# Dilation of four graphs: one drop, one check and one set of right sides for a quad, with ranks scaled by a reciprocal

## The reference

```
h = h @ W + b;  nh = h / max(norm(h), EPS)
cos = nh @ nh.T;  ew = edge_weight * cos
h = ew @ h            (relu but for the last)
```

```
row = carry[n];  num = sum(row)
sf = where(num > 10, (num + 1) // 2, 1)
rm = row & (cumsum(row) % sf == 0)
rm = where(mask[n] != 0 and num > 1, rm, False)
carry[n] = row & ~rm;  carry[:, n] = carry[:, n] & ~rm
```

## Time and profile before

| | us |
|---|---|
| median of 3 runs | 3010.84 |
| lowest, highest | 3008.5, 3018.25 |
| the profiled execution, its own time | 3018.62 |
| its span, first to last instruction | 3016.8 |
| PE busy in the span | 2784.0 (92%) |
| DVE busy | 2277.1 (75%) |
| ACT busy | 1251.4 (41%) |
| POOL busy | 1082.2 (36%) |

### The profile page before, as it was taken

One profiled execution on the slowest core, in us unless ns is written; L12 is line 12 of the kernel. 1 busy time (PEld: TensorE's weight loads), 2 busy tenths in 40 slices (PEclk: granted clock), 3 DMA queues, 4 the chain that ended last, 5 costly groups with the idle time before them and its releaser, 6 DMA issues. The chain is left out here.

```text
span 3016.8 us, 41011 instructions
## 1 busy us (share of the span) xinstructions
PE 2784.0 (92%) x13446; PEld 1740.0 (58%) x13446; DVE 2277.1 (75%) x6124; ACT 1251.4 (41%) x3652; POOL 1082.2 (36%) x493
## 2 busy tenths in 40 slices
PE   6988999998999998899998997799999979999997
PEld 4655656655555655556655564455555545555786
DVE  4788998888988898898888886766566524676567
ACT  2544541545541554541554530233332224443564
POOL 4534333434333232321000000776666612443661
PEclk9999999999999999999999998899999989999998
DMA  6446336446327345326214102355554516996653
GB/s 215 134 136 206 105 99 213 137 130 210 109 84 227 113 133 192 105 62 190 91 57 164 60 15 98 128 212 215 191 188 181 189 70 242 396 395 270 241 200 126
DMA packets 304077, 492.27 MB, mean 163 GB/s; under 512 B 18544, under 2 KB 196080, under 8 KB 303856
## 3 DMA queue, kind: packets, MB, share of 16 engines
q1 hardware_dynamic: 303856, 489.57, 46.8%
HBM read 422.38 MB, written 67.11 MB: 162 GB/s over the span
## 5 line engine op out<-in xcount | busy, mean ns | idle before, releaser
L478 POOL TENSOR_SCALAR a_AT<-a_ats 128x512 uint8<-128x512 f32 x256 | 504.2, 1974 | 871.2 <-DMA a_ats<-in_adjT 809.3
L538 PE MATMUL a_acc<-a_ew,a_Hr 128*128 128x512 f32 x1536 | 796.0, 600 | 3.1 <-ACT a_hT L626 3.1
L717 DVE TENSOR_TENSOR a_ew<-adj,a_cos 128x512 f32<-128x512 f32 x768 | 522.6, 681 | 146.4 <-PE a_cos L531 145.2
L529 PE MATMUL a_cos<-a_nh 128*128 128x512 f32 x768 | 447.3, 582 | 2.4 <-DVE a_nl L709 2.4
L1286 POOL TENSOR_TENSOR b_dsum<-adj 128x1024 f32<-128x1024 f32 x16 | 141.9, 8870 | 662.2 <-DVE adj L1240 662.2
L538 PEld LDWEIGHTS a_acc<-a_ew,a_Hr 128*128 128x128 f32 x1536 | 292.3, 191 | 73.3 <-DVE a_ew L717 3.6
L640 ACT ACTIVATE a_vr<-a_D,a_sm_b,a_sm_sc 128x128 f16<-128x128 f32 x560 | 210.6, 456 | 246.0 <-DVE a_sm_b L766 245.4
L531 PE MATMUL a_cos<-a_nh,a_nl 128*128 128x512 f32 x768 | 306.3, 399 | 0.0
L530 PE MATMUL a_cos<-a_nl,a_nh 128*128 128x512 f32 x768 | 305.9, 398 | 0.0
L1130 PE MATMUL b_acc<-adj,b_h 128*128 128x512 f32 x512 | 224.3, 596 | 22.5 <-DVE adj L1240 22.5
L1290 POOL TENSOR_TENSOR b_dsum<-b_dsum,adj 128x1024 f32<-128x1024 f32 x96 | 225.8, 2352 | 14.1 <-POOL b_dsum L1290 0.5
(11 more groups left out here) (204 smaller groups left out, 4756.6 us busy)
## 6 DMA issues: line engine op xcount, KB each, us to landing
adj<-in_adjT SPq DMA_DIRECT2D x108, 1024.0 KB, 12.7
adj<-in_adjT SPq DMA_DIRECT2D x128, 512.0 KB, 5.8
a_ats<-in_adjT SPq DMA_DIRECT2D x256, 256.0 KB, 3.4
a_af<-in_adj SPq DMA_DIRECT2D x256, 256.0 KB, 3.4
scr_keep<-a_kp SPq DMA_DIRECT2D x128, 128.0 KB, 1.8
b_kp<-scr_keep SPq DMA_DIRECT2D x16, 1024.0 KB, 8.2
c_zi<-scr_z SPq DMA_DIRECT2D x32, 512.0 KB, 6.1
c_ai<-scr_ag SPq DMA_DIRECT2D x32, 512.0 KB, 7.0
```

Source lines behind the costliest of these rows:

```text
L478: e.tensor_scalar(AT[i][:, 4 * h:4 * h + 4, blk(k)].bitcast(U8), ats[h][:], 0.0, ONE8, ALU.is_gt, ALU.mult).then_inc(T["at"], 1)
L529: e.matmul(cos[j][:], n[:, blk(k)], n[:, half(j)], start=True, stop=False)
L538: e.matmul(acc[j][:], Hr[u % 2][:, k, :], ew[idx % 3][:], start=(k == 0), stop=(k == NK - 1)).then_inc(E["agg"], 1)
L717: e.tensor_tensor(ew[idx % 3][:], adj[g % 2][:, k, half(j)], cos[j][:], ALU.mult).then_inc(E["ew"], 1)
```

## The change

The small tiles of four graphs become one tile with an axis for the graph (AT, R, Ab, Au, X, Sd, v8), and the values of the rule lie in one tile `small`. Three steps that were four operations become one of 128x512: the drop, the check, and the pair Au and X. For the drop a single number has to be compared for all four graphs, where sf was a column for each. So the rule computes iv = 1/sf, and ACT's scale is sc = min(iv, 1) * g: vr then equals 1 where it equalled sf. The same holds for row_out, whose column sf becomes the constant 1.0. The pair Au and X leaves the start and is a stage of its own, cross, of width 0.6, after the fourth start. The again of PE waits once, for the one drop.

```diff
@@ DilationPlan
             for i in range(Q):
                 add(1, "start", n, i)
+            add(0.6, "cross", n)
             for r in range(K):
...
 def ticks(n, r):
-    return 9 * round_of(n, r) + n + (1 if r else 0)
+    return 10 * round_of(n, r) + n + (1 if r else 0)
@@ pe, again
                     for i in range(Q):
-                        if i % 2 == 0:
-                            e.wait_ge(T["vr"], Q * rr + i + 2)
-                        e.wait_ge(T["sd"], Q * rr + i + 1)
-                        count(i, Sd[i][(r + 1) % 2][:])
+                        if i == 0:
+                            e.wait_ge(T["sd"], rr + 1)
+                        count(i, Sd[(r + 1) % 2][:, i, :])
@@ pe, wide
                     if i == 0:
-                        e.wait_ge(T["vr"], Q * rr + (2 if j == 0 else 4))
+                        e.wait_ge(T["sd"], rr + 1)
...
-                    if j == 0:
-                        e.wait_ge(T["sd"], Q * rr + i + 1)
@@ dve, start
-                    e.wait_ge(T["sign"], 8 * n + 2 * i + 2)
-                    if i:
-                        e.wait_ge(T["x"], Q * n + i)
-                    e.scalar_tensor_tensor(Au[:], ab[:, blk(k)], 0.0, C["tri"][:], ALU.max, ALU.mult,
-                                           saturate=False).then_inc(T["au"], 1)
-                    e.wait_ge(T["au"], Q * n + i + 1)
-                    e.scalar_tensor_tensor(X[i][:], AT[i][:, k, blk(k)], 2.0, Au[:], ALU.mult, ALU.subtract,
-                                           saturate=False).then_inc(T["x"], 1)
+                elif kind == "cross":
+                    n, = a
+                    k, first = n % NK, Q * (n % 2)
+                    if n:
+                        e.wait_ge(T["v8"], n)
+                    e.wait_ge(T["sign"], 8 * n + 8)
+                    e.scalar_tensor_tensor(Au[:], Ab[:, first:first + Q, blk(k)], 0.0,
+                                           C["tri"][:].unsqueeze(1).to_broadcast([128, Q, 128]), ALU.max, ALU.mult,
+                                           saturate=False).then_inc(T["au"], 1)
+                    e.wait_ge(T["au"], n + 1)
+                    e.scalar_tensor_tensor(X[:], AT[:, :, k, blk(k)], 2.0, Au[:], ALU.mult, ALU.subtract,
+                                           saturate=False).then_inc(T["x"], 1)
@@ dve, rule
-                    e.scalar_tensor_tensor(sm["sc"][:], flat4, 10.5, mv, ALU.is_gt, ALU.mult).then_inc(T["ru"], 1)
-                    e.scalar_tensor_tensor(sm["va"][:], flat4, 1.5, mv, ALU.is_gt, ALU.mult).then_inc(T["ru"], 1)
+                    e.scalar_tensor_tensor(sm["g"][:], flat4, 10.5, mv, ALU.is_gt, ALU.mult).then_inc(T["ru"], 1)
                     e.wait_ge(T["ru"], t0 + 2)
                     e.tensor_scalar(sm["sf"][:], sm["t"][:], MAGIC, MAGIC, ALU.add, ALU.subtract).then_inc(T["ru"], 1)
-                    e.wait_ge(T["ru"], t0 + 3)
+                    e.scalar_tensor_tensor(sm["va"][:], flat4, 1.5, mv, ALU.is_gt, ALU.mult).then_inc(T["ru"], 1)
+                    e.wait_ge(T["ru"], t0 + 4)
+                    e.reciprocal(sm["iv"][:], sm["sf"][:]).then_inc(T["ru"], 1)
+                    e.wait_ge(T["ru"], t0 + 5)
+                    e.scalar_tensor_tensor(sm["h"][:], sm["g"][:], -4.0, sm["va"][:], ALU.mult, ALU.add).then_inc(T["ru"], 1)
+                    e.wait_ge(T["ru"], t0 + 6)
+                    e.scalar_tensor_tensor(sm["sc"][:], sm["iv"][:], 1.0, sm["g"][:], ALU.min, ALU.mult).then_inc(T["ru"], 1)
+                    e.wait_ge(T["ru"], t0 + 8)
                     e.tensor_tensor(sm["c"][:], sm["sc"][:], base0, ALU.mult).then_inc(T["ru"], 1)
-                    e.wait_ge(T["ru"], t0 + 4)
-                    e.scalar_tensor_tensor(sm["h"][:], sm["sc"][:], -4.0, sm["va"][:], ALU.mult, ALU.add).then_inc(T["ru"], 1)
-                    e.wait_ge(T["ru"], t0 + 7)
-                    e.tensor_tensor(sm["b"][:], sm["sf"][:], sm["h"][:], ALU.mult).then_inc(T["ru"], 1)
-                    e.wait_ge(T["ru"], t0 + 8)
-                    e.tensor_tensor(sm["b2"][:], sm["b"][:], sm["c"][:], ALU.add).then_inc(T["ru"], 1)
+                    e.wait_ge(T["ru"], t0 + 9)
+                    e.tensor_tensor(sm["b2"][:], sm["c"][:], sm["h"][:], ALU.add).then_inc(T["ru"], 1)
@@ dve, drop
-                    for i in range(Q):
-                        e.wait_ge(T["vr"], Q * rr + i + 1)
-                        e.scalar_tensor_tensor(Sd[i][(r + 1) % 2][:], vr[:, i, :], sm["sf"][:, i:i + 1], X[i][:],
-                                               ALU.is_equal, ALU.is_lt, saturate=False).then_inc(T["sd"], 1)
+                    e.wait_ge(T["vr"], Q * rr + Q)
+                    e.scalar_tensor_tensor(Sd[(r + 1) % 2][:], vr[:], 1.0, X[:], ALU.is_equal, ALU.is_lt,
+                                           saturate=False).then_inc(T["sd"], 1)
@@ dve, check
+                    e.scalar_tensor_tensor(Au[:], Sd[0][:], 1.0, Sd[1][:], ALU.mult, ALU.not_equal,
+                                           accum_out=C["flags"][:, n:n + 1], saturate=False).then_inc(T["v8"], 1)
@@ dve, row_out
-                    e.scalar_tensor_tensor(R[i][:, k, half(j)], v[c % 3][:], sm["sf"][:, i:i + 1],
+                    e.scalar_tensor_tensor(R[:, i, k, half(j)], v[c % 3][:], 1.0,
```

More of the change, by code:

```diff
@@ L386, in layer0 @@
         ss, s2, s3, rn = (P.sb(n, [128, NK]) for n in ("rnss", "rns2", "rns3", "rnrn"))
-        AT = [P.sb(f"AT{i}", [128, NK, N], FP8) for i in range(Q)]
-        R = [P.sb(f"R{i}", [128, NK, N], FP8) for i in range(Q)]
+        AT = P.sb("AT", [128, Q, NK, N], FP8)
+        R = P.sb("R", [128, Q, NK, N], FP8)
         ats = [P.sb(f"ats{i}", [128, 4, 128]) for i in range(2)]
         af = [P.sb(f"af{i}", [128, 512]) for i in range(3)]
-        Ab = [P.sb(f"Ab{i}", [128, N], FP8) for i in range(2 * Q)]
-        Au = P.sb("Au", [128, 128], FP8)
-        X = [P.sb(f"X{i}", [128, 128], FP8) for i in range(Q)]
-        Sd = [[P.sb(f"Sd{i}{j}", [128, 128], FP8) for j in range(2)] for i in range(Q)]
-        v8 = P.sb("v8", [128, 128], FP8)
+        Ab = P.sb("Ab", [128, 2 * Q, N], FP8)
+        Au = P.sb("Au", [128, Q, 128], FP8)
+        X = P.sb("X", [128, Q, 128], FP8)
+        Sd = [P.sb(f"Sd{j}", [128, Q, 128], FP8) for j in range(2)]
+        v8 = P.sb("v8", [128, Q, 128], FP8)
         base = P.sb("base", [128, 2, 2, 2])
@@ L402, in layer0 @@
         kp = [P.sb(f"kp{i}", [128, N], FP8) for i in range(2)]
-        sm = {n: P.sb(f"sm_{n}", [128, Q]) for n in ("t", "sf", "sc", "va", "h", "b", "c", "b2")}
+        small = P.sb("small", [128, 9, Q])
+        sm = {n: small[:, x, :] for x, n in enumerate(("t", "sf", "iv", "g", "sc", "va", "h", "c", "b2"))}
         Dp = P.ps("D", [128, 2, 512])
@@ L550, in pe @@
                     for q in others:
-                        e.matmul(rank(i)[:, 132:134], AT[i][:, q, blk(k)], (C["two1"] if q < k else C["zero1"])[:],
+                        e.matmul(rank(i)[:, 132:134], AT[:, i, q, blk(k)], (C["two1"] if q < k else C["zero1"])[:],
                                  start=(q == others[0]), stop=(q == others[-1]))
-                    count(i, AT[i][:, k, blk(k)])
+                    count(i, AT[:, i, k, blk(k)])
                 elif kind == "again":
@@ L633, in act @@
                         e.wait_ge(T["rw"], 8 * (n - 2) + 2 * i + 2)
-                    e.activation(Ab[Q * (n % 2) + i][:, half(j)], af[r % 3][:], ACT.Sign,
+                    e.activation(Ab[:, Q * (n % 2) + i, half(j)], af[r % 3][:], ACT.Sign,
                                  saturate=False).then_inc(T["sign"], 1)
@@ L637, in act @@
                     n, r = a
-                    e.wait_ge(T["ru"], ticks(n, r) + (10 if r == 0 else 9))
+                    e.wait_ge(T["ru"], ticks(n, r) + (11 if r == 0 else 10))
                     for i in range(Q):
@@ L650, in act @@
                     e.activation(v[c % 3][:], Dp[:, j, :], ACT.Abs,
-                                 bias=b1[:, i:i + 1] if j else sm["b"][:, i:i + 1],
+                                 bias=b1[:, i:i + 1] if j else sm["h"][:, i:i + 1],
                                  scale=sm["sc"][:, i:i + 1]).then_inc(T["av"], 1)
@@ L655, in act @@
                             e.wait_ge(T["av"], 8 * (n - 1) + 2 * i + 2)
-                        e.activation(b1[:, i:i + 1], Dp[:, 0, 511:512], ACT.Identity, bias=sm["b"][:, i:i + 1],
+                        e.activation(b1[:, i:i + 1], Dp[:, 0, 511:512], ACT.Identity, bias=sm["h"][:, i:i + 1],
                                      scale=sm["sc"][:, i:i + 1]).then_inc(T["b1"], 1)
@@ L804, in dve @@
                         e.wait_ge(T["tr"], 2 * m + j + 1)
-                        e.scalar_tensor_tensor(kp[m % 2][:, half(j)], Dp[:, j, :], 0.5, R[i][:, q, half(j)],
+                        e.scalar_tensor_tensor(kp[m % 2][:, half(j)], Dp[:, j, :], 0.5, R[:, i, q, half(j)],
                                                ALU.is_lt, ALU.is_gt, saturate=False).then_inc(T["kp"], 1)
```

25 lines of the change are left out of this document (7 added, 18 removed).

## The result

| | before | after |
|---|---|---|
| median of four runs, us | 3010.76 | 3116.43 |
| lowest, highest | 3008.5, 3018.25 | 3109.91, 3122.72 |
| ratio | | 1.0346 (1.0318 to 1.0374) |
| profiled execution, its span | 3018.62, 3016.8 | 3109.91, 3108.1 |
| DVE busy in the span | 2277.1 (75%) | 2174.8 (70%) |

The changed kernel is 3.5% slower. The forecast of 3044 us had the sign right, and 3116 lies above its whole range. DVE lost 102 us of work, and the time grew by 105. Behind layer 0 nothing changed: 1153 to 1154 us from there to the end of the span, both times.

The account below looks back on a forecast made before the run. In layer 0 PE and DVE are both near their limit, and ACT paces the drops in most rounds. 34 + 38 + 10 - 20 - 14 - 12 - 3 = +33 us on 3010.84 gives 3044 us, range 2990 to 3085.

Parts of the forecast that it names:

- absorbed: DVE's idle time in the rounds, waiting for cos, eats part of the delays: -20 us.
- The picture of the loop: Layer 0 rounds: ACT's Abs pace the drops; the new loop needs 4.3 us, PE's work 3.5 us a round.
- Part 3: PE's four counts after the drop all come after one semaphore, the last one 0.17 us later: +10 us.
- Part 4, Au and X: Merged pair in its own slot: 42 us of DVE instead of 68, half of the saving in PE-late starts: -12 us.
- Part 4, the check: Four check operations become one, 19 us less on DVE; its slot is then PE's, so -14 us kept.
- Part 1: Rule block on DVE: ten operations and a longer chain, 1.35 us instead of 1.11, 140 times: +34 us.
- Parts 2 and 3: Merged drop waiting for the fourth Abs, +38 us, and PE's counts after one semaphore, +10 us.
- Parts 1 to 3: Rule block, drop and counts in the rounds of layer 0 together: +82 us gross.
- The clock rival: PE's longer gaps in the rounds double the time at 1.2 GHz: some +25 us more, 3070 us; chance 0.1.
- The column of 256 row_out: row_out drops its column scalar, 15 us in all at the middle value, mostly hidden by waits for PE: -3 us.
- 82 - 11 - 40 - 50: Nearly even rival: delays absorbed twice as much, cheaper merged operations, full Part 4 savings: about 3005 us; chance 0.13.

Follow-up runs that it names:

- e13: e12 with the one merged drop of the change, counts and first wide waiting for it: 3060.08 us, 1.0149.
- e12: e10 with a rule of eleven small operations, one more, whose chain is one step shorter: 3004.54 us, 0.9966.
- e9: e5 with each first wide matmul waiting only for its own graph's drop: 3039.85 us, 1.0082.
- e5: e2 with the stage cross at width 0: 3060.14 us, 1.0147.
- e6: The kernel before with the change's new rule alone (ten operations, comparisons with 1.0), four drops and four checks: 3027.48 us, 1.0037.
- e10: e9 with Au and X computed for each graph in its start again and no stage cross: 3026.41 us, 1.0034.
- e2: The changed kernel with four drops of 128x128, PE's counts each waiting for their own: 3074.21 us, 1.0195.
- e1: The changed kernel with the stage cross at width 0 instead of 0.6: 3100.47 us, 1.0284.
- e11: The kernel before with Sd merged and one check of 128x512 instead of four: 3018.08 us, 1.0018.
- e4: The kernel before with an empty stage of width 0.6 after each block's fourth start: 3041.81 us, 1.0091.
- e7: The changed kernel with rule and drop widths of 1.15 instead of 0.9: 3083.02 us, 1.0231.

## Why the prediction was right in sign and wrong in size

| part | forecast, us | by the runs, us | which |
|---|---|---|---|
| drop and counts in the rounds | +48 | +36 | e13 against e12, stretch of the rounds |
| first wide waits for all four | 0 | +15 to +20 | the same, wide stretch; e9 against e5 |
| rule, with what its constant gives back | +34, -3 | +11 | e6 |
| Au and X merged, in a lump | -12 | +14 | e10 against e9 |
| width of the stage cross | 0 | +14 to +19 | e2 against e5, after against e1 |
| check merged | -14 | 0 to +5 | e11 |
| absorbed | -20 | in the rows above | |
| sum | +33 | +90 to +105 | measured +105 |

Taken one after the other from the changed kernel the steps close: cross at width 0 19 us, four drops 41, the wide's own waits 20, Au and X in the starts 14. These are 94 of the 105. What is left is e10, 10 us behind the kernel before, with the new rule and the merged check, and e6 with the rule alone has +11.

**Right.** The picture of the loop. The drop takes 0.69 us (forecast 0.68 to 0.76) and ends 0.73 us behind the last Abs, 0.34 later than four did (forecast 0.37). The rule block takes 1.36 (1.35). The shortest round with two slots is 4.14 (4.3): the counts and the way back to DVE take 0.52, not 0.68. The drop waits for a_vr in 116 rounds (120), for 133 us, above the 100 to 115. DVE's busy time fell by 102 us (80) without any gain, and the stages behind are unchanged. The sentence of the Trainium skill that speaks against the change ("Perfetto Trace Analysis", Optimizing Scalar/DVE Operations: where Vector isn't saturated but makes bubbles on other engines, breaking up instructions may let work be completed sooner) was the right one; the traces agree at 1, 2 and 4 pieces with 4.14, 3.87 and 3.73 us a round.

**The step of Part 3 that stopped too early.** "now all four come after one semaphore" was followed for the counts (L490) only. The wide matmuls wait on the same `sd`, and the diff changes their wait too. The view of the earlier trace rows had the row for it, 5.2 us at L575, but it is small just because the wide starts early, and I left it out. It needed a look at one last drop and the wide behind it, as above: 0.64 us ahead of its end. 15 to 20 us were missing. The +10 that Part 3 did put down isn't seen: from the last drop to the next rule block it is 0.52 us before and after.

**Part 4, Au and X: the wrong sign.** I summed DVE's work, 68 us against 42, and said that half of it was covered. The measured sign is the other one, +14 instead of -12. In the start shown DVE waits for cos, and it is PE that is late, so four small pairs can be free where a lump in a stage of its own is not. The text even had the reason ("start slots in which PE is late anyway") and then took a price for the merged pair as if it lay in the same slots.

**Part 4, the check.** The forecast kept 14 of 19 us. The measured gain is none. In the kernel before, PE starts the wide while DVE is still in its drops and is busy beside the check, which would cover DVE's work there; that reading wasn't tested by itself, and why merging may even lose 3 to 8 us is open.

**The stage without instructions.** "the cross now stands in a slot of its own" read the width as where the work stands. In this planner a width is also a share of 768 slots taken from all others. The forecast had no term for it; e4 prices it at 27 us in the kernel before with nothing in it, and e1 at 19 in the changed one. Which of the moved slots costs the time stays open.

**Part 1, too dear.** The duration was right, its sum of +34 was not the net: the same edit takes the column out of every drop, which shortens the paced loop by 0.06 us a round, 8 us in all. The prediction saw the column's price for row_out only (0 to 0.08, and the trace gave 0.06), and there it put down -3 of 15. Of the 27 us left in the rounds 15 came through in e6.

**Absorbed.** 20 of 82 us were to vanish in DVE's idle time. Of the shorter rule 17 and 21 of 25 us came through, of the longer one in e6 15 of 27, and of Parts 2 and 3 36 of 48. In sum the allowance was about right, in part by luck, since it splits otherwise than Parts 1 to 3 say.

**The clock rival.** It was given 3070 us if the time at the 1.2 GHz level doubled, for 25 us more. By the clock records of the traces it did double: 51 us up to the last mask before, 102 after. But it costs little here. These are PE's costliest groups, the matmuls of a_acc, before, after and in e4:

```profile
L538 PE MATMUL a_acc<-a_ew,a_Hr 128*128 128x512 f32 x1536 | 796.0, 600 | 3.1 <-ACT a_hT L626 3.1
```

```profile
L540 PE MATMUL a_acc<-a_ew,a_Hr 128*128 128x512 f32 x1536 | 804.2, 606 | 2.3 <-ACT a_hT L625 2.2
```

```profile
L539 PE MATMUL a_acc<-a_ew,a_Hr 128*128 128x512 f32 x1536 | 801.7, 604 | 1.9 <-ACT a_hT L627 1.9
```

With the three lines of a_cos added, the matmuls of the 768 slots are 14 us longer in PE's busy time after than before, 6 us in e4, and 4 us shorter in e13 than in e12. So by the profile, which models the ends of matmuls, the clock carries some 14 of the 105 us, 6 of e4's 27, and nothing of the merged drop's 55. The rest of the added time is idle time of PE. Inside the rounds the time at the lower level is 14 us before and 17 in e5; it is 37 in e2 (slots out), 41 in e1 (merged drop) and 63 after (both). So each of the two edits comes with a lower clock in the rounds, by about as much; which of PE's gaps bring it down was not looked at. e12 and e13 have 10 and 21.

**Sums that don't come out.** The column of 256 row_out at the middle value, 0.04 us, is 10 us and not 15, which is 0.06. 82 - 11 - 40 - 50 is -19, not -15. The ends of the forecast's own terms add up to -8 to +77, which is 3003 to 3088 and not 3010 to 3080. None of these reaches 3116.

The rows of the table miss 0 to 15 us of the measured 105, as the parts were measured on different bases: the merged drop gives 41 us between e5 and e1 and, without the wide's part, 36 on the fastest kernel. e7 shows that the loss also depends on how the widths fit.

## What to carry to other kernels

When several small operations are merged into one, ask for each input when it is ready and for each user when it starts: behind the slower producer here the last piece of four ends 0.3 us after it, the merged one 0.7, and a later user of the semaphore can pay as well, not only the next in line. A busy total that falls says nothing about the time: in each stretch look first at who is late there; work that lies in another engine's shadow is free in pieces and may be dear in a lump. In a schedule that deals out slots by weights, a new stage has a price even if it is empty, and a changed loop needs its weights set anew.

## What the runs showed of the hardware that was not expected

- A column as the scalar of a DVE operation costs 0.06 us against a constant: 763 against 701 ns at 128x512, 371 against 313 ns at 128x128 (the same fp16 and fp8 tiles, means over 256 and 560).
- The reciprocal of 128x4 takes 178 ns, as much as a product or a sum of two tiles of that size (177 and 178).
- In a block of 128x4 operations a dependent step weighs more than an operation: ten in a chain of seven take 1.37 us, eleven in a chain of six 1.19, nine in a chain of five 1.11.
- PE's time at the 1.2 GHz level in the rounds went from 14 to 63 us, and to 40 by an empty stage alone, which only spaces the same matmuls differently. The matmuls of the slots got only 14 and 6 us longer by it.
